# The first attention's stacks fetched by columns on three queues, and its closing made by chunks of tokens in the last group's steps

## The reference

```python
def _L0_attn_ref(x, Wq, bq, Wk, bk, Wv, bv, Wo, bo):
    q = split_heads(x @ Wq + bq)
    k = split_heads(x @ Wk + bk)
    v = split_heads(x @ Wv + bv)
    att = jnp.einsum('bhqd,bhkd->bhqk', q, k) * scale
    att = jnp.where(mask, att, jnp.float32(-jnp.inf))
    att = jax.nn.softmax(att, axis=-1)
    y = jnp.einsum('bhqk,bhkd->bhqd', att, v)
    return y @ Wo + bo
...
x = x + _layernorm(_L0_attn_ref(_layernorm(x, axis=-1), ...), axis=-1)
x = x + _layernorm(_L0_ffn_ref(_layernorm(x, axis=-1), ...), axis=-1)
```

## Time and profile before

| | us |
|---|---|
| median of 3 runs (2608.78 to 2621.18) | 2617.71 |
| the profiled execution | 2606.84 |
| its span | 2605.0 |
| TensorE busy / VectorE busy | 2248.0 / 2042.2 |
| ScalarE busy / GpSimd busy | 1713.8 / 908.6 |

### The profile page before, as it was taken

How to read it: one execution, slowest core, us unless ns; L and a number is a source line. 1 busy time by engine, 2 the same in 40 slices (tenths; PEclk the granted TensorE clock), 3 DMA queues, 4 the chain that set the end, 5 groups by cost and what they waited for, 6 DMA issues and landing times. The chain is left out here.

```text
span 2605.0 us, 93094 instructions
## 1 busy us (share of the span) xinstructions
PE 2248.0 (86%) x36506; PEld 1449.7 (56%) x36660; DVE 2042.2 (78%) x2644; ACT 1713.8 (66%) x3577; POOL 908.6 (35%) x502
## 2 busy tenths in 40 slices
PE   2158989899469999999989998999989999899994
PEld 1023333332237766767666666767667676676764
DVE  5248777674568888888878888888888888888884
ACT  1034566567357877777777777777767777777773
POOL 4100000000044545454444444444444444444440
PEclk8579999999789999999999999999999999999996
DMA  3410111100001112111121111211121111211110
GB/s 103 60 46 2 21 20 21 20 2 1 1 23 30 35 27 56 47 33 29 39 55 37 32 30 48 55 28 34 28 55 47 31 31 29 62 39 31 31 30 22
DMA packets 63521, 89.38 MB, mean 34 GB/s; under 512 B 20278, under 2 KB 31492, under 8 KB 63060
## 3 DMA queue, kind: packets, MB, share of 16 engines
q1 hardware_dynamic: 62470, 81.90, 13.9%
q0 software_dynamic: 608, 1.37, 0.2%
HBM read 28.48 MB, written 4.39 MB: 13 GB/s over the span
## 5 line engine op out<-in xcount | busy, mean ns | idle before, releaser
L668 POOL TENSOR_TENSOR arena<-arena 128x1024 f32<-128x1024 f32 x192 | 465.8, 2426 | 937.4 <-ACT arena L744 937.4
L719 ACT ACTIVATE arena<-bank 128x512 f32<-128x512 f32 (+3 forms) x640 | 316.9, 551 | 312.3 <-PE bank L912 162.4
L1210 DVE TENSOR_REDUCE arena<-bank 128x1 f32<-128x1024 f32 (+7 forms) x384 | 335.5, 908 | 178.0 <-PE bank L889 135.3
L985 PEld LDWEIGHTS bank<-ident,arena 128*128 128x128 f32 x3072 | 339.8, 142 | 184.2 <-issue 114.4
L769 ACT ACTIVATE arena<-bank 128x512 f32<-128x512 f32 x768 | 418.3, 603 | 23.5 <-PE bank L985 19.9
L985 PE MATMUL bank<-ident,arena 128*128 128x128 f32 x3072 | 419.9, 279 | 13.3 <-DVE arena L1320 8.3
L979 PE MATMUL bank<-wqk,arena 128*128 128x512 f32 x768 | 388.7, 630 | 28.8 <-issue 15.1
L685 POOL TENSOR_TENSOR arena<-arena 128x1024 f32<-128x1024 f32 x96 | 182.3, 1899 | 628.7 <-ACT arena L744 628.7
L744 ACT ACTIVATE arena<-bank 128x1024 f32<-128x1024 f32 x192 | 196.5, 1024 | 296.3 <-PE bank L979 293.4
L1307 DVE TENSOR_REDUCE arena<-arena 128x16 f32<-128x1024 f32 x192 | 233.4, 1216 | 144.2 <-POOL arena L674 140.2
L908 PE MATMUL bank<-arena 128*128 128x512 bf16 (+3 forms) x611 | 198.3, 363 | 63.5 <-DMA arena<-max_parts 54.0
(11 more groups left out here) (148 smaller groups left out, 3524.2 us busy)
## 6 DMA issues: line engine op xcount, KB each, us to landing
arena<-arena SPq DMA_DIRECT2D x768, 64.0 KB, 2.0
arena<-qk_parts SPq DMA_DIRECT2D x72, 128.0 KB
wqk<-in_L_ffn_Wqkv SPq DMA_DIRECT2D x12, 512.0 KB, 3.7
qk_parts<-arena SPq DMA_DIRECT2D x6, 512.0 KB, 2.6
wv<-in_L_ffn_Wqkv SPq DMA_DIRECT2D x6, 512.0 KB, 4.3
wo<-in_L_ffn_Wo SPq DMA_DIRECT2D x6, 512.0 KB, 4.0
w<-in_L_ffn_W SPq DMA_DIRECT2D x6, 341.0 KB, 3.2
out<-x SPq DMA_DIRECT2D x1, 1024.0 KB, 5.1
```

The lines of the kernel that those rows point to most:

```text
L668: gp.tensor_tensor(rots[:, s], raw_qk[:, s], tab(l, t, s, 1).to_broadcast([P, H, DH]), ALU.mult).then_inc(done, 1)
L719: act.activation(ring[:, u % 8, lo:QC], bank[:, 4 + u % 3, lo:QC], ACT.Exp, scale=SCALE1).then_inc(exp_done, 1)
L985: last = pe.transpose(bank[:, out + b, P * (i % 4):P * (i % 4) + P], src[:, i].rearrange("p h d -> p (h d)"), ident[:, :])
L1210: ve.tensor_reduce(pmax[:, m, c:c + 1], src, AX.X, ALU.max).then_inc(piece_read, 1)
```

## The change

Queries and keys get a tile each and go block by block of 512 columns: projected, evicted, split, and written out as six pieces per block, with a semaphore per block. Group 0's stack is fetched in three chunks of columns, 0 to 511, 512 to 1023 and 1024 to 2047, the query side on SyncE's queue and the key side on ScalarE's; TensorE waits for a chunk at the first "max" piece that needs it. The stacks of groups 1 to 3 are fetched on GpSimd's queue, behind its table. SyncE does the shifts next, and the first layer's weights and biases after the last of them. The planner's 200 that becomes 600 leaves the old steps in their order.

The closing is cut in four chunks of 512 tokens with three new steps: "yT" (transpose `kept`, VectorE copies), "z" (times Wo, then `close` on VectorE) and "xT" (transpose, VectorE writes `resid`). Those of chunks 0 to 2 stand among the last group's steps 26 to 39, those of chunk 3 behind the last "out". The inverse root is Ln and Exp on ScalarE, set between its exponentials. GpSimd clears `kT` and `vv`. The old closing over 16 blocks on all engines goes. Some tiles move in the arena so that nothing still in use is overwritten. Of the diff, what is only taken away, and was told above, is left out in places.

```diff
+CLOSE = 26
+CHUNKS = ((0, 1), (1, 2), (2, 4))
...
-    exp_end, part_end, pv_end, unit_end, stack_end = [], [], [], {}, {0: 0, 1: 200}
+    exp_end, part_end, pv_end, unit_end, stack_end = [], [], [], {}, {0: 0, 1: 600}
...
+    after = [(CLOSE, "yT", 0)]
+    for c in range(NQC - 1):
+        if c + 1 < NQC - 1:
+            after.append((CLOSE + 4 * c, "yT", c + 1))
+        after += [(CLOSE + 4 * c + 1, "z", c), (CLOSE + 4 * c + 5, "xT", c)]
+    for s, what, c in sorted(after, key=lambda i: (i[0], i[1] != "xT", i[2])):
+        at = next((n for n, i in enumerate(order) if i == (NHG - 1, "score", s, 0)), len(order) - 1)
+        order.insert(at, (NHG - 1, what, c))
+    order += [(NHG - 1, what, NQC - 1) for what in ("yT", "z", "xT")]
...
+        def stack(eng, g, slot, sides, lo, hi, done):
+            for s in sides:
+                dst = kst if s else qst
+                for i in range(3):
+                    for j in range(3):
+                        r = (3 * i + j) * D1
+                        part = qk_parts[s, j if s else i].rearrange("(g h d) t -> d g h t", g=NHG, h=HG)
+                        eng.dma_start(dst[r:r + D1, bass.ds(slot, 1), :, lo:hi], part[:, bass.ds(g, 1), :, lo:hi]).then_inc(done, 16)
+        def clear_maxima(eng, slot, done):
+            eng.dma_start(qst[ROWS:ROWS + 3, bass.ds(slot, 1)],
+                          a["c_zeros"].rearrange("r (s h t) -> r s h t", s=1, h=HG)).then_inc(done, 16)
+        def ones_row(eng, slot, done):
+            eng.dma_start(kst[ROWS:ROWS + 3, slot], a["c_ones"].rearrange("r (h t) -> r h t", h=HG)).then_inc(done, 16)
...
-            for s, p3 in ((0, parts_q), (1, parts_k)):
-                for i in range(3):
-                    sp.wait_ge(parts_ready, 3 * s + i + 1)
-                    sp.dma_start(qk_parts[s, i], p3[i]).then_inc(parts_out, 16)
-            sp.wait_ge(parts_out, 96)
...
-            def stack(g, slot):
-                for i in range(3):
-                    for j in range(3):
-                        r = (3 * i + j) * D1
-                        for s, n, dst in ((0, i, qst), (1, j, kst)):
-                            src = qk_parts[s, n].rearrange("(g h d) t -> d g h t", g=NHG, h=HG)[:, bass.ds(g, 1)]
-                            sp.dma_start(dst[r:r + D1, bass.ds(slot, 1)], src).then_inc(stack_in, 16)
...
-                sp.dma_start(qst[ROWS:ROWS + 3, bass.ds(slot, 1)],
-                             a["c_zeros"].rearrange("r (s h t) -> r s h t", s=1, h=HG)).then_inc(stack_in, 16)
+            def parts(b):
+                cols = slice(QC * b, QC * b + QC)
+                for s, p3 in ((0, parts_q), (1, parts_k)):
+                    for i in range(3):
+                        sp.wait_ge(parts_ready, 6 * b + 3 * s + i + 1)
+                        sp.dma_start(qk_parts[s, i, :, cols], p3[i][:, cols]).then_inc(parts_out[b], 16)
...
-            for s in range(2):
-                sp.wait_ge(stack_clear, 2 * (s + 1))
-                sp.dma_start(kst[ROWS:ROWS + 3, s], a["c_ones"].rearrange("r (h t) -> r h t", h=HG)).then_inc(ones_in, 16)
-                stack(s, s)
-                sp.wait_ge(ones_in, 16 * (s + 1))
-                sp.wait_ge(stack_in, 16 * NSTACK * (s + 1))
+            sp.wait_ge(stack_clear, 2)
+            ones_row(sp, 0, first_in[0])
+            clear_maxima(sp, 0, first_in[0])
+            for c, (lo, hi) in enumerate(CHUNKS):
+                for b in range(lo, hi):
+                    parts(b)
+                for b in range(lo, hi):
+                    sp.wait_ge(parts_out[b], 96)
+                stack(sp, 0, 0, (0,), QC * lo, QC * hi, first_in[c])
+            for k, what, *i in order:
+                if what == "turn":
+                    maxima(k, k % 2, i[0])
...
-            for k, what, *i in order:
-                if what == "turn":
-                    maxima(k, k % 2, i[0])
-                elif what == "pv" and i[0] == NS - 1 and k + 2 < NHG:
-                    sp.wait_ge(pv_done, NS * (k + 1))
-                    stack(k + 2, k % 2)
...
+            ones_row(gp, 1, ones_in)
+            for g in range(1, NHG):
+                if g >= 2:
+                    gp.wait_ge(pv_done, NS * (g - 1))
+                stack(gp, g, g % 2, (0, 1), 0, T, stack_in)
+                clear_maxima(gp, g % 2, stack_in)
+            gp.wait_ge(oT_read, NHG * NQC)
+            gp.memset(kT, 0.0).then_inc(tiles_clear, 1)
+            gp.memset(vv, 0.0).then_inc(tiles_clear, 1)
...
+            for b in range(4):
+                for s, raw in ((0, raw_q), (1, raw_k)):
+                    act.wait_ge(qk_ready, 2 * b + s + 1)
...
+            act.wait_ge(stack_clear, 2)
+            for c, (lo, hi) in enumerate(CHUNKS):
+                for b in range(lo, hi):
+                    act.wait_ge(parts_out[b], 96)
+                stack(act, 0, 0, (1,), QC * lo, QC * hi, first_in[c])
...
+                    if k == NHG - 1 and s > CLOSE and (s - CLOSE) % 2 == 0:
+                        if (s - CLOSE - 2) // 2 < 2 * (NQC - 1):
+                            scale((s - CLOSE - 2) // 2)
+            def scale(i):
+                c = slice(4 * (i // 2), 4 * (i // 2) + 4)
+                act.wait_ge(mean_square, i + 1)
+                act.activation(stat[:, 5, c], stat[:, 4, c], ACT.Ln).then_inc(mean_log, 1)
+                act.wait_ge(mean_log, i + 1)
+                act.activation(stat[:, 2, c], stat[:, 5, c], ACT.Exp, scale=-0.5).then_inc(scale_ready, 1)
+            act.add_instruction(mybir.InstLoadActFuncSet(name=nc.get_next_instruction_name(), act_func_set_id=6))
...
+            for i in range(2 * (NQC - 1), 2 * NQC):
+                scale(i)
+            act.wait_ge(small_ready, 1)
...
-                        pe.wait_ge(ones_in, 32)
-                    pe.wait_ge(stack_in, 16 * NSTACK * (g + 1))
+                        pe.wait_ge(ones_in, 16)
+                    if g:
+                        pe.wait_ge(stack_in, 16 * NSTACK * g)
+                if g == 0 and (h, t % 4, c) == (0, 0, 0):
+                    for n, (first, _) in enumerate(CHUNKS):
+                        if first == u:
+                            pe.wait_ge(first_in[n], 16 * (18 + 2 * (n == 0)))
...
+                elif what == "yT":
+                    c = i[0]
+                    if c == 0:
+                        pe.wait_ge(piece_read, NHG * NPC)
+                    pe.wait_ge(oT_read, NQC * k + c + 1)
+                    wait(pe, yT_read, c)
+                    for t in range(4):
+                        last = pe.transpose(bank[:, 0, P * t:P * t + P], kept[:, 4 * c + t, :], ident[:, :])
...
+                elif what == "z":
+                    c = i[0]
+                    pe.wait_ge(yT_read, c + 1)
+                    wait(pe, z_read, c)
+                    for t in range(4):
+                        last = mm(bank[:, 1, P * t:P * t + P], y1T[:, c % 2, P * t:P * t + P], w_in[:, 3, :],
+                                  start=True, stop=True)
...
+                elif what == "xT":
+                    c = i[0]
+                    pe.wait_ge(x_norm, 4 * c + 4)
+                    wait(pe, resid_ready, 2 * c)
+                    for t in range(4):
+                        last = pe.transpose(bank[:, 2, P * t:P * t + P], x[:, 4 * c + t, :], ident[:, :])
...
+            pe.wait_ge(small_ready, 1)
+            pe.wait_ge(tiles_clear, 2)
...
+            for b in range(4):
+                cols = slice(QC * b, QC * b + QC)
+                for s, raw, p3 in ((0, raw_q, parts_q), (1, raw_k, parts_k)):
+                    ve.wait_ge(qk_read, 2 * b + s + 1)
+                    for i in range(3):
+                        ve.tensor_copy(p3[i][:, cols], raw[:, cols]).then_inc(parts_ready, 1)
+                        if i < 2:
+                            ve.wait_ge(parts_ready, 6 * b + 3 * s + i + 1)
+                            step(ve.tensor_tensor(raw[:, cols], raw[:, cols], p3[i][:, cols], ALU.subtract))
...
+            def close(b):
+                c = slice(4 * b, 4 * b + 4)
+                each = lambda s: stat[:, s, c].unsqueeze(2).to_broadcast([P, 4, C])
+                def chunk_norm(i, src, dst):
+                    step(ve.tensor_reduce(stat[:, 0, c], src, AX.X, ALU.add))
+                    step(ve.tensor_scalar(stat[:, 1, c], stat[:, 0, c], -1.0 / C, None, ALU.mult))
+                    step(ve.tensor_tensor(dst, src, each(1), ALU.add))
+                    step(ve.tensor_tensor(zsq[:, c], dst, dst, ALU.mult))
+                    step(ve.tensor_reduce(stat[:, 3, c], zsq[:, c], AX.X, ALU.add))
+                    ve.tensor_scalar(stat[:, 4, c], stat[:, 3, c], 1.0 / C, EPS, ALU.mult, ALU.add).then_inc(mean_square, 1)
+                    ve.wait_ge(scale_ready, i + 1)
+                ve.wait_ge(z_ready, b + 1)
+                ve.tensor_tensor(z[:, c, :], bank[:, 1, :].rearrange("p (t c) -> p t c", t=4),
```

(25 more changed lines are left out.)

92 lines of the change are left out of this document (23 added, 69 removed).

## The result

The changed kernel takes 2521.81 us (median of 4 runs, 2520.07 to 2525.26), the kernel before beside it 2618.19 (2608.78 to 2621.18). The ratio is 0.9636, 95% interval 0.9615 to 0.9657: 96 us won. The forecast was 2520. The profiled execution took 2520.07 us with a span of 2518.3, 86.7 less than the span before; the two figures differ because the profiled execution before was 11 us quicker than its median, and the one after 1.7.

What follows compares the result with a forecast made beforehand. TensorE was held by shifts queued behind stacks on SyncE's queue and by the closing. Gains 62 - 2 + 13 + 17 = 90 off the profiled 2606.8 gave 2516.8, plus 3 for the median: 2520 us, range 2490 to 2556.

Steps and rivals of the forecast that it cites:

- The first stack: Start of the attention: group 0's stack in chunks brings the first score to 92 us from 153.6, gain 62.
- has landed by 49: Group 0's stack: chunk 0, first transfer at 36.6 us, is in by 49, including 2.5 us of landing.
- far from 88: Sign of failure at the start: chunk 2 of group 0's stack lands far from 88 us.
- 92 against 74: First score: 92 us if two queues add nothing, about 74 if they carry twice as much.
- estimate of 54 GB/s: Stack transfers: eight partitions reach two of 16 DMA ports, 54 GB/s by the skill's 436 for all.
- GpSimd's stacks: Groups 1 to 3: 40 us a stack; stack 1's traffic loses 2 us, shifts freed from SyncE's queue gain 13.
- under 10: Later groups' shifts return in under 10 us with stacks on GpSimd's queue, where a delayed one took 31.5.
- The closing: End of attention: 32.6 us won behind the last output, 16 lost inside the last steps, net gain 17.
- (a): Rival: the three queues are one, shifts stand behind GpSimd's stacks; 77 us won, 2533; chance 0.12.
- (b): Rival: transfer time goes by descriptor, each chunk of the first stack costs 40 us; 10 won; chance 0.07.
- (c): Rival: the closing stalls the last steps by 31 us instead of 16; 75 won, 2535; chance 0.10.
- (d): Rival: GpSimd's stacks are slow, at 120 us each 104 us lost, 2621 to 2631; chance 0.03.

Runs made afterwards that it cites:

- kernel with four edits: Changed kernel: unit 0's shifts ahead of chunk 2's query half, GpSimd's clears and stack 1 issued later, each closing xT one step later; 2497.86 us.
- one-queue kernel: Changed kernel with both sides of the three chunks on SyncE's queue, none on ScalarE's; 2515.84 us (one run).

## Why the prediction was right

**The forecast held** (2520 against 2521.8), by its mechanisms, with errors that cancel in part. In spans: start 72.1 for 62, shifts 8.6 for 11, closing 15.7 for 17, together 96.4 for 90; the layers took back 9.7, for which the prediction had no term. The 3 us that it allowed between the profiled execution and the median were 1.7.

**The first stack** was the term mis-sized. First maximum: 54.5 for 56.8, because the 3.3 us copy of vcur was really 0.46 us and a collision. The chunks: the step "has landed by 49", then parts, 63.5, 66, 88.5, added 2.5 us of landing to each chunk and to the parts. In the queue, transfers follow without it: the issues of the chunks stand at 36.38, 47.64 and 59.13, 11.4 us apart where I had 14.4 and 15, and chunk 2 took 19.9 for 22.5. So the shifts came through at 79, not 88.5, and the score at 81.5, not 92. A chunk 2 "far from 88" was named as a sign of failure; 9.5 us off, it shows a wrong size and not a wrong mechanism, since the shifts still stood behind it. That VectorE's shifts would be ready (68.7 for 68.4) but would stand behind chunk 2 was right, and the kernel with four edits shows what that place was worth: up to 9.4 us, with VectorE ready 2.8 sooner.

**Two queues do not add.** The prediction kept 92 against 74 on the ground that both sides go to the same rows; that was right, and the one-queue kernel goes further: for chunk 2 the second queue was no help at all (19.9 us against 15.6). The estimate of 54 GB/s beside it does not hold as a bound, though: every stack of eight-partition transfers ran faster, from 61 to 125 GB/s.

**GpSimd's stacks** were right in sign and wrong in the numbers: 24 and 21 us long, not 40 (242.12 to 266.02 and 366.01 to 387.19, bounds by the shifts that come through next), at a share of 0.97 to 1.08; "about half the DMA engines are busy whoever issues" was wrong. This made the price of stack 1's traffic 6 us of waiting (0 to 6, taken as 2) and the delay of later shifts 9.8 and 12.7 us, where "under 10" was asked for; both are hidden, and the 13 us came whole. The step I did not take is the turned loop: with the old order of GpSimd's stacks the changed kernel is at 2541, still in the range, with 20.5 us of waiting behind stack 1. That the forecast came within 2 us is therefore in part luck: a part of the change that it did not price brought some 19 us, and it priced these stacks at 40 us with only 2 us of harm.

**The closing** was right in nearly each piece: 13.2 us of insertion up to step 39's exponentials and 2.2 more from these to the last output (5.28 us for 3.05), together 15.5 for 15.5; the xT waits 2.34, 2.34 and 2.87 for about 1.6 to 2.8, ScalarE's pauses 3.66 and 2.77 for 3 to 4. Behind the last output it took 17.9 us (609.27 to 627.19) for 16.5. The 2.2 and most of this 1.4 are TensorE at the lower level of its granted clock, 1.2 GHz: it was at 1.00 until about 602, stood idle from 599.8 to 602.6 waiting for chunk 2's norm, and was at 0.50 from then on (the window below), where the last steps before the change ran at 1.00 up to the last output. The products with Wo took 2.08 us here for the 1.2 in the sum, and 1.05 in chunk 0, at the upper level.

```profile
561.06 1.05 PE L1014 MATMUL bank<-w_in,arena 128*128 128x128 f32 x8
...
611.17 2.08 PE L1014 MATMUL bank<-w_in,arena 128*128 128x128 f32 x8 [0.78 <-DVE arena L1351]
```

```profile
605.00:627.20 22.20, 6.73 (x37) 4.43 (x33) 12.97 (x30) 1.31 (x6) 5.68 (x2) 0.50 0.00 0
```

**The rivals**: (a) fell with the stacks put back on SyncE's queue, (b) with the chunks themselves, 11.4 us apart where it had 40 each, and with the single chunk, (c) with the closing alone, (d) with stacks of 21 to 24 us.

## What to carry to other kernels

A small transfer that someone waits for costs what is queued ahead of it: look in the queue's rows for it between a long issue and its own landing, and move it ahead of the large one before making the large one faster. When transfers write only a few partitions, let neighbours in the queue go to different ones, and don't expect a second queue that writes the same partitions to double the rate. Read a loop that a change turns as a change of its own. And where a short operation takes ten times its usual time in one place, look at what GpSimd does at that moment before its price goes into a sum.

## What the runs showed of the hardware

While eight-partition transfers run, the mean busy share of the 16 DMA engines is 0.47 to 0.53 when SyncE or ScalarE issue them and 0.96 to 1.09 when GpSimd does. The Trainium skill (DMA: Bandwidth & Descriptors, Issuing engines are not separate DMA queues) says that all issuers use the same 16 DMA engines and that starting transfers from several of them saves only issue time; for these transfers who issues mattered more than that, 65 to 83 GB/s from SyncE against 109 to 125 from GpSimd in the same order. A 12 KB transfer takes 1.4 us alone, 7.4 to 13.4 beside a stack of another queue in the new order, up to 25 beside one in the old order, and 29.8 to 35.1 when it is issued within 3 us behind a stack of its own queue. Two transfers in a row to the same eight partitions cost rate: 114 against 69 GB/s from GpSimd, 15.6 against 19.6 us for the same chunk from SyncE.
